# Narrow norm sums spread by DMA, no loop, and the key-value products on DVE, in a one-core RWKV-7 layer with experts

## Chip, cores and metric

One core of one Trainium2 chip runs the whole kernel. The metric is the time of one execution on the device, in microseconds (us). Its engines are TensorE (PE, matrix products; PEld is its weight load), VectorE (DVE), ScalarE (ACT), GpSimd (POOL) and SyncE (SP), which only issues DMA transfers. Each engine runs its own instructions in program order, and they wait for one another by semaphores.

## The reference

The input x has 16 sequences of 512 tokens with 128 channels, that is 16 heads of 8 channels. One layer of RWKV-7 comes first, then a top-1 mixture of 4 experts.

```python
x = _ln(x, ...); xn = _ln(x, ...)              # two layer norms over 128 channels
xr, xw, xk, xv, xa, xg = xn + (_shift(xn) - xn) * x_r, ...
r = xr @ W_r; k = xk @ W_k; v = xv @ W_v
w_log = -softplus(-(w0 + tanh(xw @ w1) @ w2)) - 0.5
a = sigmoid(a0 + xa @ a1 @ a2); g = sigmoid(xg @ g1) @ g2
kk = (k * k_k) / norm(k * k_k over each head); k = k * (1 + (a - 1) * k_a)
def step(state, inp):                          # 512 steps, state is 8x8 for each sequence and head
    sa = einsum('bhij,bhj->bhi', state, a_t)
    state = state * d_t + sa * b_t + v_t * k_t
    return state, einsum('bhij,bhj->bhi', state, r_t)
o = _gn_heads(o) + (r * k * r_k).sum(-1) * v   # norm over each head's 8 channels
x = x + (o * g) @ W_o
x = x + square(relu(kf @ W_ffn1)) @ W_ffn2     # kf: layer norm and shift of x
# then: layer norm, router, top-1 expert of 4 (128 to 512, gelu, 512 to 128), add, layer norm
```

## The kernel before

Channels lie on the 128 partitions. A tile of 512 columns holds one chunk: 32 tokens (steps) of 16 sequences. There are 16 chunks and so 512 steps, each of which needs the state of the one before.

**One step** of the scan is four operations in a ring, on tiles of 128 columns. DVE forms `s_a` = state x a_t (L769). PE sums it over each head into `sa_ps` (L338). DVE forms `upd` = sa_ps x b_t (L775) and the next `state` = upd + plus_kv (L779). Beside it POOL forms `plus_kv` = state + kv (L965) for the same step. The product of values and keys, `kv`, is made ahead of time for a quarter of a chunk (8 steps) by `spread_kv` (L930), in four parts of 256 columns on POOL, at every odd step of the quarter before. Its values come from `val_rep`: SP copies `val_c` over the partitions with 8 DMAs for each quarter (`replicate`, L253). POOL also forms `s_r` = state x r_t at every even step (L957), which PE gathers into `o_ps` (L331), 8 products of 128 columns at steps 3, 11, 19 and 27.

**Everything else** (norms, projections, feed-forward, experts) is done for whole chunks, in slices between the steps: the front of the next chunk and the back of the two before. The table `AT` gives each item a step relative to its chunk's first; item `at` of chunk c stands in every engine's program at step `at` mod 32, between `s_a` and `upd` on DVE, behind the step's `sa_ps` product on PE, behind `plus_kv` on POOL (`pipeline`, L221). ACT and SP have no scan work, so for them `AT` sets only the order. A late input of such an item holds up the scan behind it.

**Norms.** Six times in a chunk (the layer norms `rs0`, `rs1`, `frs`, `ers`, `lrs`, and `rk`, the norm of kk) ACT squares 512 columns, PE sums them over the channels with a full 128x128 weight (`j0`, `j1`, `fj`, `ej`, `lj`, `kks`), which repeats the sum on all partitions, and ACT takes Ln and Exp of all 512 columns (`rsqrt`, L514) into `rs_p`, `rs_m` or `rs_f`. A seventh norm, `grs`, is over heads.

**The loop.** Chunks -1 to 3 and 14 to 17 are written out, chunks 4 to 13 run in a hardware loop of 5 passes over two chunks (L237); -1, 16 and 17 are the fill and drain of the pipeline. Before the first item PE, ACT and POOL wait for all 37 constants (L302, L512, L927), among them the weights that PE transposes and centres (L303 to L319).

Of the kernel before, what the change touches and what calls it, by code (L numbers as in the profile page):

```python
# [25 lines left out]
LOOP_START = 4  # L26

AT = {
    "c0": -32, "x_in": -29, "sq0": -28, "j0": -23, "rs0": -22, "x1": -21, "xh0": -20, "c1": -20, "sq1": -20,
    "j1": -19, "rs1": -17, "xh1": -17, "xn": -15, "dx": -15, "wa": -14, "mix_r": -14, "mix_k": -13, "k": -13,  # L30
    "th_w": -12, "mix_v": -12, "key": -12, "w2": -12, "th_d": -12, "val_c": -11, "mix_g": -11, "rk": -11,
    "v": -10, "kks": -10, "k2": -10, "val_sb": -10, "p": -10, "val": -9, "cum": -9, "rep": (-9, 11, 12, 15),
    "r": -8, "rec": -8, "g1": -8, "kk": -8, "rkb": -7, "k_t": -7, "kki": -7, "a_t": -7, "rkb_ps": -5,
    "th_g": -4, "r_t": -4, "bonus": -4, "g2": -1, "b_t": 0, "bonus_b": 0, "gate": 1, "gsq": 29, "grs": 33,
# [11 lines left out]
CONSTS = 37  # L46
# [60 lines left out]
def build(nc, xT, mats, vecs, consts, b1_in, out):  # L107
    with ExitStack() as ctx:
# [36 lines left out]
        def v(name):  # L145
# [14 lines left out]
        sq_p, lv_p, rs_p, xh_p = (sb(n, COLS) for n in ("sq_p", "lv_p", "rs_p", "xh_p"))  # L160
# [60 lines left out]
        def pipeline(eng, work, scan_step=None):  # L221
# [23 lines left out]
        def _(sp):  # L245
# [4 lines left out]
            for n in range(3):  # L250
                sp.dma_start(b1_rows[32 * n:32 * n + E, :], b1_in).then_inc(s["w_in"], 16)
# [812 lines left out]
```

## Time and profile before

| | |
|---|---|
| median of 3 runs | 1262.86 us (1260.15 to 1266.98) |
| the profiled execution | 1263.76 us, its span 1261.6 us |
| busy share of the span | PE 85%, DVE 70%, POOL 67%, ACT 53% |
| first step of the scan begins | 63.4 us |
| scan ends | 1184.8 us |
| mean granted clock of TensorE | 0.912 of full speed |

The span counts from the first instruction of the program to the last. An engine's share is an average over a start, 16 chunks and a tail. Since the scan is a ring of four dependent operations, the view that tells most is the timeline between one `s_a` and the next: it shows which engine the ring waited for in that step.

### The profile page before, as it was taken

The numbers are of one execution on the slowest core, as the hardware profiler recorded it, in microseconds if no ns is written. First come the engines' busy times: TensorE is split into PE (matmuls) and PEld (weight loads), VectorE is DVE, ScalarE is ACT, GpSimd is POOL, SyncE is SP. The second block draws the span as 40 slices with busy tenths as digits, with TensorE's granted clock in tenths as the row PEclk, the third lists the DMA queues.
The fourth block names the chain that finished last, engine by engine and source line by source line (L and its number), as shares of the span: only waits on it lengthen the run. The fifth ranks groups of instructions, "written<-read, shape, count | busy, mean of one in ns | idle before, by whom it ended". The sixth has DMA issues, their size and how long they took to land.

```text
span 1261.6 us, 17218 instructions
## 1 busy us (share of the span) xinstructions
PE 1069.5 (85%) x4211; PEld 528.6 (42%) x4211; DVE 878.1 (70%) x2155; ACT 665.9 (53%) x967; POOL 845.0 (67%) x1141
## 2 busy tenths in 40 slices
PE   2556688989898998989799998989899998988877
PEld 1133334444444444444444444444444444444433
DVE  3256686877878686877778786787778687876421
ACT  1524173746566383746557383647557383744352
POOL 0167676868777776878677776878677677877210
PEclk9967598989899898989899897989899898989898
DMA  2222212131312212031311212131311213131000
GB/s 103 39 37 51 34 36 35 17 73 17 69 25 53 40 17 63 15 74 17 72 21 45 47 17 59 17 75 17 64 28 44 48 17 64 17 63 17 17 9 8
DMA packets 81165, 49.87 MB, mean 40 GB/s; under 512 B 9148, under 2 KB 74684, under 8 KB 80968
## 3 DMA queue, kind: packets, MB, share of 16 engines
q1 hardware_dynamic: 81096, 49.17, 19.7%
q14 instruction: 52, 0.43, 0.1%
q8 instruction: 17, 0.28, 0.1%
HBM read 11.38 MB, written 4.19 MB: 12 GB/s over the span
## 4 chain that ended last, share of the span: by engine, by line
PE 66%; DVE 22%; issue 6%; ACT 4%; DMA 1%; SPq 0%; POOL 0%; DVEq 0%; ACTq 0%; POOLq 0%
PE sa_ps L338 12%; PE pre_a L298 9%; PE fin_a L479 8%; PE fin_b L479 8%; PE pre_b L298 6%; DVE state L779 6%; DVE s_a L769 5%; DVE upd L775 4%; PE mid_ps L298 4%; PE fin_b L488 3%; PE mid_ps L433 3%; PE fin_a L298 2%; PE o_ps L331 2%; PE fin_b L457 1%; PE fin_b L298 1%
## 5 line engine op out<-in xcount | busy, mean ns | idle before, releaser
L965 POOL TENSOR_TENSOR plus_kv<-state,kv 128x128 f32<-128x128 f32 x512 | 282.0, 551 | 258.2 <-DVE state L779 233.2
L338 PEld LDWEIGHTS sa_ps<-s_a,con 128*128 128x128 f32 x1024 | 191.1, 208 | 352.0 <-DVE s_a L769 267.6
L338 PE MATMUL sa_ps<-s_a,con 128*128 128x128 f32 x1024 | 242.8, 322 | 82.1 <-DVE s_a L769 79.6
L775 DVE TENSOR_TENSOR upd<-sa_ps,b_t 128x128 f32<-128x128 f32 x512 | 147.9, 289 | 198.5 <-PE sa_ps L338 190.0
L942 POOL TENSOR_TENSOR kv<-val_rep,k_t 128x256 f32<-128x256 f32 x256 | 232.4, 908 | 33.3 <-DMA val_rep<-val_c 33.3
L957 POOL TENSOR_TENSOR s_r<-state,r_t 128x256 f32<-128x256 f32 x256 | 225.3, 880 | 1.3 <-DVE state L779 1.3
L779 DVE TENSOR_TENSOR state<-upd,plus_kv 128x128 f32<-128x128 f32 x512 | 190.1, 371 | 19.4 <-POOL plus_kv L965 2.0
L769 DVE TENSOR_TENSOR s_a<-state,a_t 128x128 f32<-128x128 f32 x512 | 177.0, 346 | 19.1 <-DVE state L779 1.7
L479 PE MATMUL fin_b<-h_e,mat 128*128 128x512 f32 x256 | 133.3, 630 | 2.0 <-ACT pick L678 2.0
L508 ACT ACT_TABLE_LOAD x103 | 132.1, 1283 | 1.8
L479 PE MATMUL fin_a<-h_e,mat 128*128 128x512 f32 x256 | 126.5, 599 | 0.0
L678 ACT ACTIVATE pick<-fin_b 68x512 bf16<-68x512 bf16 x16 | 9.5, 592 | 145.9 <-PE fin_b L465 145.9
L633 ACT ACTIVATE sq_m<-o_ps 128x512 f32<-128x512 f32 x16 | 9.6, 597 | 132.2 <-PE o_ps L331 132.2
L488 PE MATMUL fin_b<-act,mat 128*128 128x512 f32 x128 | 66.4, 604 | 0.0
L479 PEld LDWEIGHTS fin_b<-h_e,mat 128*128 128x128 f32 x256 | 48.1, 207 | 42.2 <-issue 39.4
L433 PE MATMUL mid_ps<-hid,mat 128*128 128x512 f32 x128 | 65.5, 594 | 0.3 <-ACT hid L663 0.3
L685 ACT ACTIVATE act<-fin_b 128x512 f32<-128x512 f32 x32 | 19.0, 595 | 79.6 <-PE fin_b L482 79.6
L479 PEld LDWEIGHTS fin_a<-h_e,mat 128*128 128x128 f32 x256 | 44.1, 190 | 36.2 <-issue 33.0
L298 PE MATMUL pre_b<-sq_p,con 128*128 128x512 f32 x96 | 53.5, 641 | 3.0 <-ACT sq_p L526 2.1
L298 PE MATMUL mid_ps<-z_m,mat 128*128 128x512 f32 x96 | 51.0, 614 | 1.3 <-DVE z_m L862 1.3
L983 POOL TENSOR_TENSOR k<-key,k 128x512 f32<-128x512 f32 x16 | 23.0, 1441 | 35.4 <-ACT k L592 35.4
L331 PE MATMUL o_ps<-s_r,con 128*32 128x128 f32 x1024 | 43.0, 288 | 0.0
(189 smaller groups left out, 1791.9 us busy)
## 6 DMA issues: line engine op xcount, KB each, us to landing
val_rep<-val_c SPq DMA_DIRECT2D x512, 64.0 KB, 2.4
x_in<-xT SPq DMA_DIRECT2D x16, 256.0 KB, 2.8
x_res<-xT SPq DMA_DIRECT2D x16, 256.0 KB, 2.9
outT<-res SPq DMA_DIRECT2D x16, 256.0 KB, 2.0
mat<-mats SPq DMA_DIRECT2D x1, 2306.0 KB
con<-consts SPq DMA_DIRECT2D x1, 584.0 KB, 3.6
hid<-b SPq DMA_DIRECT2D x3, 8.0 KB
vec<-vecs SPq DMA_DIRECT2D x1, 11.5 KB, 3.6
```

What stands on the lines that cost most here:

```text
L298: return mm(bank_, lhsT, rhs, start=True, stop=True).then_inc(s[name], 1)
L338: mm(sa_ps[:, 0:STATE], k("sum8"), s_a[:], start=True, stop=True).then_inc(s["sa"], 1)
L433: last = mm(mid_ps[:], w("ffn2", j), hid[j][:], start=(j == 0), stop=(j == J - 1))
L479: mm((fin_b, fin_a)[j % 2][:], mat[:, M["W1"] + e * I + j * C:M["W1"] + e * I + (j + 1) * C], h_e[e][:], start=(e == 0), stop=False)
L488: last = mm(fin_b[:], w("Wo", j), act_j[j][:], start=(j == 0), stop=(j == J - 1))
L508: nc.scalar.preload_act_table_set(name)
L769: tt(ib(s_a[:]), ib(st(t)), over_i(a_t[c.slot][:, t * B:(t + 1) * B]), ALU.mult).then_inc(s["s_a"], 1)
L775: tt(ib(upd[:]), ib(sa_ps[:, 0:STATE]), over_i(b_t[c.slot][:, t * B:(t + 1) * B]), ALU.mult).then_inc(s["upd"], 1)
L779: tt(st(t + 1), upd[:], plus_kv[:, (t % 2) * STATE:(t % 2 + 1) * STATE], ALU.add).then_inc(s["state"], 1)
L942: tt(to, values, keys.unsqueeze(1).broadcast_to([128, 2, QUARTER, B]), ALU.mult).then_inc(s["kv"], 1)
L957: tt(part, states, r.unsqueeze(2).broadcast_to([128, 2, N, B]), ALU.mult).then_inc(s["s_r"], 1)
L965: tt(plus_kv[:, (t % 2) * STATE:(t % 2 + 1) * STATE], st(t), kv[:, at:at + STATE], ALU.add).then_inc(s["plus_kv"], 1)
```

## The change

Five things are changed.

1. **Narrow sums.** The six norms' sums are taken with weights of 32 columns (`mean32`, `sum8k`), four products of 128 columns side by side on the four column groups of PE (`sums`). The result for 512 columns lies on 128 partitions x 128 columns. ACT takes Ln and Exp of 128 columns (`rsqrt_row`) into a small tile, and SP spreads it over the channels with four DMAs (`over_channels`). DVE then waits for these.
2. **No loop.** All iterations are written out.
3. **kv on DVE.** `spread_kv` moves from POOL to DVE, in two halves of 512 columns, at steps 2 and 5 of each quarter.
4. **Start.** `x` is loaded first, the small tiles are filled before the constants arrive, and the weights are turned and centred (`turn_weights`, `center_weights`, `weights`) behind the first items of chunk 0, no longer ahead of them.
5. **A new table** `AT`. `grs` also moves to the bank `mid_ps`.

```diff
+    "c0": -32, "j0": -31, "x_in": -31, "sq0": -30, "rs0": -29, "d_rs0": -24, "xh0": -24, "x1": -24, "c1": -22,
...
+    "gg": 39, "wo": 40, "x2": 41, "fc": 41, "fsq": 41, "fj": 42, "frs": 43, "xf": 45, "d_frs": 45, "x2x": 47,
...
-            with eng.Fori(LOOP_START, LOOP_START + RING * (loops - 1) + 1, RING) as first:
...
+            for c in range(FIRST, LAST + 1):
                 iteration(Chunk(0, c))
...
+            def over_channels(c, name, to, free=(), heads=None):
...
+                sp.wait_ge(s["row_" + name], now)
+                for g in range(4):
...
+                        rows = row[name][32 * g:32 * g + 32, :].unsqueeze(1).broadcast_to([32, 4, QCOLS])
+                        sp.dma_start(to[:, g * QCOLS:(g + 1) * QCOLS], rows).then_inc(s[name], 16)
...
+            def sums(bank_, first, which, of, name):
+                for g in range(4):
+                    last = mm(bank_[32 * g:32 * g + 32, first:first + QCOLS], k(which, 0, 32),
+                              of[:, g * QCOLS:(g + 1) * QCOLS], start=True, stop=True, skip_group_check=True)
...
-                    one(pre_b[:], k("mean"), sq_p[:], "j0")
+                    sums(pre_b, 0, "mean32", sq_p, "j0")
+                    if not c.has(1):
+                        turn_weights()
...
+            def rsqrt_row(c, var, eps, n_in, n_ln, name, scale=1.0):
...
+                f(row[name][:], var, ACT.Ln, bias=eps, scale=scale).then_inc(s[n_ln], 1)
+                act.wait_ge(s[n_ln], c.count())
+                f(row[name][:], row[name][:], ACT.Exp, scale=-0.5).then_inc(s["row_" + name], 1)
...
+            def spread_kv(c, q, half):
...
+                tt(part, values.rearrange("p (i t b) -> p i t b", i=N // 2, t=QUARTER),
+                   keys.unsqueeze(1).broadcast_to([128, N // 2, QUARTER, B]), ALU.mult).then_inc(s["kv"], 1)
...
+                if part in (2, 5) and nxt[0].has():
+                    spread_kv(*nxt, part // 3)
```

**POOL, six steps inside a chunk, before.** `kv` is the key-value product, `s_r` the read-out; `plus_kv` is the scan's own.

```order
L957 TENSOR_TENSOR s_r<-state,r_t1 128x256 [waits s_o,s_r_t]
L965 TENSOR_TENSOR plus_kv<-state,kv 128x128 [waits s_state]
L942 TENSOR_TENSOR kv<-val_rep1,k_t1 128x2x8x16
L965 TENSOR_TENSOR plus_kv<-state,kv 128x128 [waits s_state]
L957 TENSOR_TENSOR s_r<-state,r_t1 128x256
L965 TENSOR_TENSOR plus_kv<-state,kv 128x128 [waits s_state]
L942 TENSOR_TENSOR kv<-val_rep1,k_t1 128x2x8x16 [waits s_val_rep1]
```

And now, at the same kind of place:

```order
L1003 TENSOR_TENSOR s_r<-state,r_t0 128x256
L1011 TENSOR_TENSOR plus_kv<-state,kv 128x128 [waits s_state] x2
L1003 TENSOR_TENSOR s_r<-state,r_t0 128x256 [waits s_o]
L1011 TENSOR_TENSOR plus_kv<-state,kv 128x128 [waits s_state] x2
L1003 TENSOR_TENSOR s_r<-state,r_t0 128x256
L1011 TENSOR_TENSOR plus_kv<-state,kv 128x128 [waits s_state]
```

The product is gone from between two `plus_kv`; only `s_r` is left, at every other one.

**DVE, a chunk's step 25, before.** Between `s_a` and `upd` stand the front of the next chunk (`k_t`, `mix_g`, `a_t`) and `y1` of the back.

```order
L769 TENSOR_TENSOR s_a<-state,a_t1 128x128 [waits s_state]
L820 TENSOR_TENSOR k_t0<-k2,dec_bt 128x512 [waits s_inv_p,s_k2]
L825 SCALAR_TENSOR_TENSOR mix_g<-mix_v,half_kk,dec_bt 128x512 [waits s_g1,s_inv_p,s_kk]
L829 SCALAR_TENSOR_TENSOR a_t0<-mix_v,neg_kk,p_all0 128x512 [waits s_p,s_kk]
L870 TENSOR_TENSOR y1<-mid_ps,x2x 128x512 [waits s_ec,s_y1b,s_x2x,s_f2]
L775 TENSOR_TENSOR upd<-sa_ps,b_t1 128x128 [waits s_sa]
L779 TENSOR_TENSOR state<-upd,plus_kv 128x128 [waits s_plus_kv,s_upd]
```

And now at steps 29 and 30, where the crowded step of the new order is:

```order
L824 TENSOR_TENSOR s_a<-state,a_t0 128x128 [waits s_state]
L811 TENSOR_TENSOR kv<-val_rep0,k_t1 128x4x8x16
L886 SCALAR_TENSOR_TENSOR mix_g<-mix_v,half_kk,dec_bt 128x512 [waits s_g1,s_inv_p,s_kk]
L979 SCALAR_TENSOR_TENSOR res<-y2,vec,y1b 128x512 [waits s_stored,s_y1b,s_lxh]
L834 TENSOR_TENSOR upd<-sa_ps,b_t0 128x128 [waits s_sa]
L838 TENSOR_TENSOR state<-upd,plus_kv 128x128 [waits s_plus_kv,s_upd]
L824 TENSOR_TENSOR s_a<-state,a_t0 128x128 [waits s_state]
L894 SCALAR_TENSOR_TENSOR b_t1<-dx,mix_g 128x512 [waits s_th_a,s_kki]
L834 TENSOR_TENSOR upd<-sa_ps,b_t0 128x128 [waits s_sa]
```

Where step 25 held four operations there is now one (`k_t`), and step 29 holds three, the first of them the second half of a `kv`.

**PE, steps 19 and 20, before**: the shifted projection of the next chunk (`xn` with `mat` and `wa_past`).

```order
L338 MATMUL sa_ps<-s_a,con 128x128 [waits s_s_a]
L298 MATMUL fin_a<-z_m,mat 128x512 [waits s_act,s_kf]
L298 MATMUL mid_ps<-z_m,mat 128x512 [waits s_relu,s_kf]
L338 MATMUL sa_ps<-s_a,con 128x128 [waits s_s_a]
L366 MATMUL pre_a<-xn,mat 128x512 [waits s_xh1,s_xn]
L367 MATMUL pre_a<-xn,wa_past 128x512
L338 MATMUL sa_ps<-s_a,con 128x128 [waits s_s_a]
```

And now at step 16:

```order
L363 MATMUL sa_ps<-s_a,con 128x128 [waits s_s_a]
L397 MATMUL pre_a<-xn,mat 128x512 [waits s_xh1,s_xn]
L398 MATMUL pre_a<-xn,wa_past 128x512
L511 MATMUL fin_a<-h_e1,mat 128x512
L511 MATMUL fin_a<-h_e2,mat 128x512
L363 MATMUL sa_ps<-s_a,con 128x128 [waits s_s_a]
```

The projection has moved in front of two products of the experts, and one step now holds four products of 512 columns behind the scan's own.

## Rows read from the trace of the kernel before

**Rows 1.** Four stretches: length, busy us of PE, PEld, DVE, ACT, POOL, granted clock, DMA.

```profile
203.00:273.60 70.60, 64.26 (x263) 32.19 (x262) 54.74 (x132) 40.95 (x60) 53.02 (x71) 0.94 0.22 42
...
414.20:486.90 72.70, 65.32 (x267) 32.26 (x265) 54.24 (x132) 41.42 (x61) 53.33 (x71) 0.92 0.23 44
...
1054.60:1124.10 69.50, 63.68 (x263) 31.90 (x262) 54.46 (x133) 40.94 (x60) 53.19 (x71) 0.94 0.21 39
...
1184.80:1261.60 76.80, 61.23 (x164) 26.35 (x164) 14.01 (x26) 32.09 (x44) 4.62 (x5) 0.88 0.02 7
```

**Rows 2.** Timeline of two steps at full clock: start us, us, engine, line, operation.

```profile
995.33 0.29 DVE L769 TENSOR_TENSOR s_a<-state,a_t 128x128 f32<-128x128 f32 x1
...
995.68 0.49 PE L338 MATMUL sa_ps<-s_a,con 128*128 128x128 f32 x2 [0.17 <-DVE s_a L769]
...
996.00 1.88 PE L479 MATMUL fin_a<-h_e,mat 128*128 128x512 f32 x4
...
996.86 0.29 DVE L769 TENSOR_TENSOR s_a<-state,a_t 128x128 f32<-128x128 f32 x1
...
997.72 0.39 PE L338 MATMUL sa_ps<-s_a,con 128*128 128x128 f32 x2
...
998.79 0.29 DVE L769 TENSOR_TENSOR s_a<-state,a_t 128x128 f32<-128x128 f32 x1
```

**Rows 3.** Timeline, a step with a two-input operation of 512 columns on DVE.

```profile
612.58 0.29 DVE L769 TENSOR_TENSOR s_a<-state,a_t 128x128 f32<-128x128 f32 x1
...
612.79 0.94 DVE L912 TENSOR_TENSOR y<-y,rs_f 128x512 f32<-128x512 f32 x1
...
613.15 1.17 POOL L957 TENSOR_TENSOR s_r<-state,r_t 128x256 f32<-128x256 f32 x1
...
614.50 0.29 DVE L769 TENSOR_TENSOR s_a<-state,a_t 128x128 f32<-128x128 f32 x1
```

**Rows 4.** Timeline, a product of 512 columns on POOL beside DVE.

```profile
1003.54 1.33 POOL L1001 TENSOR_TENSOR z_m<-z_m,gate 128x512 f32<-128x512 f32 x1
1003.78 1.24 DVE L769 TENSOR_TENSOR s_a<-state,a_t 128x128 f32<-128x128 f32 x1
```

**Rows 5.** DVE and POOL by line and shape, chunks 13 and 14 (984.4 to 1124.1).

```profile
L779 DVE TENSOR_TENSOR state<-upd,plus_kv 128x128 f32<-128x128 f32 x64 | 23.6, 368 | 2.2
L769 DVE TENSOR_TENSOR s_a<-state,a_t 128x128 f32<-128x128 f32 x65 | 22.8, 350 | 2.4
...
L942 POOL TENSOR_TENSOR kv<-val_rep,k_t 128x256 f32<-128x256 f32 x32 | 29.8, 932 | 3.4 <-DMA val_rep<-val_c 3.4
```

**Rows 6.** Timeline, sixteen passes of the read-out's gather on PE.

```profile
1007.43 0.65 PE L331 MATMUL o_ps<-s_r,con 128*32 128x128 f32 x16
```

**Rows 7.** Edge of the loop: timeline, and the list of waits for the whole span.

```profile
486.62 0.29 DVE L765 TENSOR_TENSOR state<-state,p_all 128x128 f32<-128x128 f32 x1 [2.72 <-issue]
...
DVE state L765 <- issue: 11.0, 4, 3.0
```

**Rows 8.** SP's transfers in the timeline, and the list of DMA issues.

```profile
603.41 5.04 SPq L265 DMA_DIRECT2D val_rep<-val_c  x8
...
val_rep<-val_c SPq DMA_DIRECT2D x512, 64.0 KB, 2.4
```

**Rows 9.** Start: timeline, and the first step in the view of tile s_a.

```profile
23.39 2.08 PE L298 MATMUL pre_a<-x_in,con 128*128 128x512 f32 x2 [0.38 <-DVE val_scan L753]
...
53.30 0.63 ACT L519 ACTIVATE rs_p<-lv_p 128x512 f32<-128x512 f32 x1
...
L769 DVE TENSOR_TENSOR s_a<-state,a_t x512: 291/292/1249, 63.4 to 1183.0; 128x128 f32<-128x128 f32 x171
```

**Rows 10.** Tail: pieces of the chain that ended last, in order of time.

```profile
1185.36 5.96 PE fin_b L479 x8
...
1256.96 0.64 ACT rs_f L519
```

**Rows 11.** Granted clock in a stretch of 2.1 us at a chunk's end.

```profile
1052.50:1054.60 2.10, 1.88 (x4) 1.11 (x5) 1.65 (x6) 0.00 (x0) 1.16 (x2) 0.50 0.00 0
```

More of the change, by code:

```diff
@@ new lines @@
+    "gate": 0, "bonus": 0, "bonus_b": 13, "x_res": 33, "gsq": 36, "gj": 36, "grs": 36, "gxh": 38, "gaff": 39,
+    "gg": 39, "wo": 40, "x2": 41, "fc": 41, "fsq": 41, "fj": 42, "frs": 43, "xf": 45, "d_frs": 45, "x2x": 47,
+    "fxh": 48, "hid": (51, 51, 55, 61), "kf": 52, "f1": (52, 53, 54, 55), "f2": (56, 57, 57, 58), "d_ers": 58,
+    "y1": 59, "ec": 59, "ej": 59, "esq": 61, "ers": 62, "h": 63, "router": 63, "best": 64, "onehot": 64,
+    "masks": 64, "h_e": (65, 65, 67, 68), "pick": 65, "y1b": 65,
@@ L157, in build @@
         xf_now, xf_past, x2x = sb("xf_now", COLS), sb("xf_past", B + COLS), single("x2x", COLS)
-        sq_p, lv_p, rs_p, xh_p = (sb(n, COLS) for n in ("sq_p", "lv_p", "rs_p", "xh_p"))
+        sq_p, rs_p, xh_p = (sb(n, COLS) for n in ("sq_p", "rs_p", "xh_p"))
+        row = {n: sb(f"row_{n}", QCOLS) for n in ("rs0", "rs1", "rk", "frs", "ers", "lrs")}
         dx = sb("dx", COLS)
@@ L358, in work @@
                     one(pre_a[:], k("center"), x1[c.slot][:], "c1")
+                    if not c.has(1):
+                        center_weights()
                 if at == AT["j1"]:
@@ L361, in work @@
                     pe.wait_ge(s["ln0"], c.count())
-                    one(pre_b[:], k("mean"), sq_p[:], "j1")
+                    sums(pre_b, 0, "mean32", sq_p, "j1")
                 if at == AT["wa"]:
+                    if not c.has(1):
+                        pe.wait_ge(s["made"], MADE)
                     pe.wait_ge(s["xn"], c.count())
@@ L418, in work @@
                 if at == AT["fj"]:
+                    if c.has(1):
+                        pe.wait_ge(s["fln"], (c + -1).count())
                     pe.wait_ge(s["fsq"], c.count())
                     pe.wait_ge(s["gln"], c.count())
-                    one(var_ps[:], k("mean"), sq_m[:], "fj")
+                    sums(var_ps, 0, "mean32", sq_m, "fj")
                 for j in range(J):
@@ L443, in work @@
                         pe.wait_ge(s["lln"], (c + -1).count())
-                    one(fin_b[:], k("mean"), sq_f[:], "ej")
+                    sums(fin_b, 0, "mean32", sq_f, "ej")
                 if at == AT["router"]:
@@ L493, in work @@
                     pe.wait_ge(s["y2"], c.count())
-                    one(fin_b[:], k("mean"), sq_f[:], "lj")
+                    sums(fin_b, 0, "mean32", sq_f, "lj")
             pipeline(nc.tensor, work, scan_step)
@@ L670, in work @@
                     tables(EXP)
[L671 to L673 removed]
+                    rsqrt_row(c, fin_b[:, 0:QCOLS], eps_ln, "ej", "eln", "ers")
                 if at == AT["pick_sb"]:
@@ L787, in work @@
                     tt(xh_p[:], pre_a[:], rs_p[:], ALU.mult).then_inc(s["xh0"], 1)
+                    if not c.has(1):
+                        weights()
                 if at == AT["xh1"]:
-                    dve.wait_ge(s["rs1"], c.count())
+                    dve.wait_ge(s["rs1"], c.count(64, 64))
                     dve.wait_ge(s["x1"], c.count())
```

291 lines of the change are left out of this document (142 added, 149 removed), and 3 rows, old and new, of the table AT.

## The prediction

> **What bounds the kernel now.** I read three views, in this order. The stretches by chunk come first [rows 1]: a chunk that is written out takes 69.5 to 70.6 us, one in the loop up to 72.7, and in both PE is busy for some 64 of them, DVE for 54, POOL for 53. No engine is full, so the ring of the scan has to be looked at step by step. The timeline of two steps is the second view [rows 2]. The first takes 996.86 - 995.33 = 1.53 us with nothing else on DVE: that is the bare ring, 32 x 1.53 = 49 us a chunk. The second has two products of 512 columns (four passes, 996.00 to 997.72, so 0.86 each) queued on PE behind the first step's `sa_ps`; the next `sa_ps` can start only at 997.72, 0.86 after its `s_a`, where it took 0.35 before, and the step takes 1.93. The other 21 us of a chunk are steps of this kind, and steps where DVE has more than fits. The third view is the timeline of such a step [rows 3]: one operation of 512 columns with two inputs in SBUF, 0.94 long beside POOL's `s_r`, makes it 1.92. POOL also stops DVE outright: beside its product of 512 columns an `s_a` takes 1.24 in place of 0.29 [rows 4]. So three engines take turns at bounding a step, and an item costs only what it adds to the longest side of its own step.
>
> **Prices from these rows.** Per step, beside the 1.53: up to 1.3 us of products on PE are free (1.53 less the 0.22 that `sa_ps` occupies), so one is free, two cost 0.4, three 1.3, four 2.1. On DVE one operation of 0.69 fits, since it lies between `s_a` and `upd`; a second costs 0.7; one of 0.94 beside `s_r` costs 0.4. A product of 512 columns on POOL costs up to 0.9.
>
> **The loop.** At an edge DVE waits 2.72 us before the carried state, and such waits sum to 11.0 us over four edges [rows 7]. Chunks 4 to 13 run from 343.3 to 1054.6, 71.1 us each; the three written-out chunks, 2, 3 and 14, take 69.9 on average. Without the loop: 10 x 1.2 = **-12 us**.
>
> **Start.** The first step begins at 63.4 us, 40 us after the first product at 23.39 [rows 9]. That product no longer waits for the weights. It needs `x` and the constants, which I put at 5.5, so 18 us go. Three norms (`rs0`, `rs1`, `rk`) now have a hop by DMA in the chain. One hop is four issues on SP of 5.04/8 = 0.63 each and 2.4 to land the last [rows 8], 3 x 0.63 + 2.4 = 4.3. Three are 13. Back come some 0.7 on ACT and 0.5 to 1.1 on PE for each, together 4 to 5. The turning of the weights on PE stands before the second sum (+2), the first quarter's `val_rep` now queues on SP behind the third hop, and `kv` and `b_t` come ahead of the first step (+2 to +4). The chain from 53.30, where `rk`'s Exp starts, shows how short the rest is. Sum: -18 + 13 - 4.5 + 2 - 1 = **-8.5 us**, first step at 55.
>
> **A chunk.** Six full sums go, 6 x 0.86 = 5.2 us of PE. Six narrow ones come. The nearest row is the read-out's gather, sixteen passes of 128 columns with 32-column weights in 0.65 at its longest and 0.58 to the next start [rows 6], so eight passes are 0.29, 1.7 us in all. PE loses 3.4 of 64 us. ACT loses 6 x 0.7 = 4, which hides. POOL loses the `kv` products, 29.8/2 = 14.9 us of 53 [rows 5]. DVE gets 8 operations of 0.69 to 0.94, 5.5 to 7.5 us. In return its `state` and `s_a`, which take 0.368 and 0.350 on average but 0.292 undisturbed [rows 5, 9], can shrink: 32 x (0.076 + 0.058) = 4.3 us at most, and only where POOL's `kv` was what disturbed them.
>
> I summed the 32 steps of both orders with the prices above, each step as the longer of its DVE and its PE side, with what PE has left over carried on. Before, this gives 68.1 us against the 69.9 measured. After, it gives 68.3. The crowded steps only move: step 25 with four operations on DVE (4.7) is gone, but step 0 holds `bonus` and the router's comparisons (3.2), 17 three mixes (3.3), 22 the scan of decays and `y2` (3.1), 29 the half `kv` and two more (3.5). On PE step 16 has four products and 7 and 21 three, where before 19, 24, 25 and 26 had three. Of the eight half `kv`, those at steps 13, 18, 21 and 29 lie beside PE work that is as long; those at 2, 10 and 26 meet `s_r` and cost 0.4 each, the one at 5 some 0.2. If none of the eight had cover they would cost 8 x 0.4 = 3.2.
>
> Waits are not in that sum. So I followed one chunk through ACT and SP too, and three inputs come late for the engine that needs them: PE at step 24 waits for the third `hid` (+0.8), PE at step 27 for the square behind `ec`, with the next `sa_ps` queued behind it (+1.2), and DVE at step 16 for `frs` (+0.9). That walk gives 68.7. The sum with its shortfall of 1.8 gives 70.1. I take the middle, 69.4, so -0.5 a chunk and, for the 14 chunks with front and back work, **-6 us**.
>
> SP issues 56 DMAs of 64 KB in a chunk, no longer 32: 56 x 0.63 = 35 of 69 us. They fit, but each hop stands in line. In the walk the margin is about 1 us for `lrs` at step 28 and `rk` at 23, 2 for `ers` at 31, over 3 for `rs0`; `rs1` at 15 comes late by 0.5 under the cover of PE.
>
> A rule of the Trainium skill bears on the POOL side. GPSIMD Engine Reference, Key points, says that GpSimd shares its SBUF interfaces with VectorE and contends with DVE instructions that have two SBUF inputs; the 1.24 of `s_a` [rows 4] agrees. It gives no price, and the same rule speaks against the change, since each `kv` on DVE is now such an instruction itself and meets `plus_kv` and `s_r`. By the rule alone the sum could fall anywhere between the 3.2 us lost and the 4.3 us gained for each chunk.
>
> **Tail.** The scan ends at 1184.8, 76.8 us before the end [rows 1]. Before, the experts of chunk 14 start 0.6 us after that [rows 10]. Now their router runs at step 31, so comparisons, masks and `pick` lie behind the scan's end: they start some 4.4 later. `frs` is covered by the experts' products, `ers` and `lrs` of chunk 15 are not: 2 x (4.3 - 0.9) = 6.8 (the last Exp at 1256.96 had only 4.6 us behind it, a hop more now). PE's narrow sums and a shorter wait for the feed-forward give 2 back. **+9 us**.
>
> **Sum.** Against the profiled execution: 1263.8 - 12 - 8.5 - 6 + 9 = 1246.3, so 1246. The median of three runs, 1262.9, is 0.9 us below that execution, so 1246 is 1.3% below it. About 0.5% is what a measurement of this kernel can tell from no change.
>
> **The rivals.**
>
> *POOL's relief counts in full.* If `state` and `s_a` shrink by half of the 4.3 us on the path, a chunk takes 67.3: 1246 - 14 x 2.1 = 1217. For it: the 512-column stops [rows 4] come where POOL runs behind. Against: most of those operations stay on POOL, and `s_r` too. 15%.
>
> *The `kv` halves have no cover and nothing comes back.* 70.4 us a chunk, +1.0: 1260, no change. For it: DVE is at 54 of 70 us [rows 1] and gets some 6 more. 17%.
>
> *The hops come late* (this one ends slower). If a hop takes 1.3 us longer than 4.3, because SP is held by a `val_rep` of 8 issues (5.04 us) or by a wait in its order, `rs1`, `frs`, `rk` and `lrs` all stop DVE, whose `upd` and so the ring stand behind them: 1.3 + 1.3 + 0.5 + 0.3 = 3.4 a chunk, 1246 + 14 x 3.4 = 1294. It decides from a lateness of about 0.6 us, where the gain is gone. Against it: SP stood idle most of the time. 15%.
>
> *PE's clock falls for longer.* At a chunk's end the granted clock is 0.50, the 1.2 GHz level [rows 11]; before it PE had little to do in steps 28 and 29. Now steps 28 to 30 hold one product each, one of them in 3.5 us, and steps 8 to 12 hold about one each. At half clock `sa_ps` gives its result 0.2 later and one product is 1.7 long, so such a step costs 0.2 to 0.6. Four or five more of them are 2 us a chunk: 1274. TensorE: Matmul & The Clock Gate, Part 1 of the Trainium skill, says that the throttled clock is the default and activity releases it; by that, taking work off PE gives something back. 10%.
>
> *The change doesn't do what it says*, `kv` on DVE standing still for `val_rep` that SP issues late: the same price as late hops, within that 15%.
>
> **Chances.** The forecast (1225 to 1256) 43%, the rivals 15, 17, 15 and 10. Low end: the first rival, 1217. High end: the clock, 1274, and half of the late hops, 1282. Faster by over 0.5% (below 1256.5): 43 + 15 and a little of the third, 60%. Within: 16%. Slower: 24%.
>
> **What would show it.** First `s_a` at 53 to 58 us; written-out chunks of 68 to 71; no DVE wait by "issue" before the carried state; `kv` on DVE at 0.69 to 0.94 mean; `rs_p`, `rs_m`, `rs_f` transfers landing 4.3 us after their first issue, with no DVE wait for them over 1 us but at step 16; a tail of 83 to 89. Chunks above 71.5, or DVE waiting for DMA in every chunk, would make me wrong.

## The result, and the profile after

The changed kernel takes **1223.4 us**, median of 4 runs (1222.3 to 1228.2); the kernel before takes 1264.1 beside it. The ratio is 0.969, with a 95% interval of 0.965 to 0.973: 3.1% faster, where 1.3% was forecast. The time lies inside the range given, but the gain is more than twice the forecast one.

The profiled execution has a span of 1221.7 us, 39.9 less than before. The first `s_a` of chunks 0, 2 and 15 and the end of the scan cut both spans into the same pieces:

| piece | before | after | difference | forecast |
|---|---|---|---|---|
| start, to the first step | 63.4 | 52.7 | -10.7 | -8.5 |
| chunks 0 and 1 | 139.6 | 132.4 | -7.2 | |
| chunks 2 to 14 | 921.1 | 885.2 | -35.9 | -18 for chunks 0 to 14, 12 of it the loop |
| chunk 15 | 60.7 | 60.7 | 0 | |
| tail | 76.8 | 90.7 | +13.9 | +9 |

The stretches of the changed kernel: its length, then the busy us of PE, PEld, DVE, ACT and POOL, the granted clock, and what the DMA did. Chunk 2, chunk 8, chunks 2 to 14 together, and the tail:

```profile
185.10:251.90 66.80, 59.07 (x299) 28.28 (x298) 58.49 (x141) 37.36 (x60) 42.44 (x55) 1.00 0.34 68
592.50:660.90 68.40, 61.57 (x299) 30.39 (x299) 58.49 (x141) 37.10 (x60) 42.45 (x55) 0.95 0.33 66
...
185.10:1070.30 885.20, 793.58 (x3873) 389.10 (x3872) 761.41 (x1820) 482.89 (x780) 551.36 (x715) 0.96 0.33 66
...
1131.00:1221.70 90.70, 64.49 (x214) 29.83 (x213) 16.34 (x36) 27.03 (x42) 4.61 (x5) 0.80 0.07 18
```

Against [rows 1], POOL went from 53 to 42 us a chunk and DVE from 54 to 58. A chunk takes 68.1 on average, where the written-out ones before took 69.5 to 70.6. Chunks 2 and 8 hold the same instructions, but chunk 2 ran wholly at the higher clock (1.00) and took 1.6 us less. The steps that differ are 1 (3.28 against 2.05) and 31 (2.22 against 1.92). What the lower clock costs is what the prediction left out, as the experiments show.

The scan's own operations on DVE and the moved product, in chunks 13 and 14 (busy us, mean ns; idle before):

```profile
L838 DVE TENSOR_TENSOR state<-upd,plus_kv 128x128 f32<-128x128 f32 x64 | 24.6, 384 | 2.2
L824 DVE TENSOR_TENSOR s_a<-state,a_t 128x128 f32<-128x128 f32 x64 | 18.7, 292 | 2.3
L811 DVE TENSOR_TENSOR kv<-val_rep,k_t 128x512 f32<-128x512 f32 x16 | 15.1, 944 | 0.0
```

`s_a` fell from 350 to its floor of 292 [rows 5]. `state` did not follow, it rose from 368 to 384. Each half of `kv` takes 0.94, the upper of the two prices given.

Where chunk 8 loses against chunk 2 is seen in the timeline (start, us, engine, line, operation). Chunk 2, steps 1 and 2, at the higher clock:

```profile
187.13 0.62 PE L489 MATMUL fin_b<-ident_bf,onehot 128*128 128x128 bf16 x8
...
187.59 0.61 PE L489 MATMUL fin_a<-ident_bf,onehot 128*128 128x128 bf16 x8
187.63 0.29 DVE L824 TENSOR_TENSOR s_a<-state,a_t 128x128 f32<-128x128 f32 x1
...
188.03 0.44 PE L363 MATMUL sa_ps<-s_a,con 128*128 128x128 f32 x2
...
189.68 0.29 DVE L824 TENSOR_TENSOR s_a<-state,a_t 128x128 f32<-128x128 f32 x1
```

The same place in chunk 8, at the lower one:

```profile
595.09 0.29 DVE L824 TENSOR_TENSOR s_a<-state,a_t 128x128 f32<-128x128 f32 x1
...
595.43 1.06 PE L489 MATMUL fin_b<-ident_bf,onehot 128*128 128x128 bf16 x8
...
596.28 1.05 PE L489 MATMUL fin_a<-ident_bf,onehot 128*128 128x128 bf16 x8
...
597.13 0.47 PE L363 MATMUL sa_ps<-s_a,con 128*128 128x128 f32 x2
...
598.37 0.29 DVE L824 TENSOR_TENSOR s_a<-state,a_t 128x128 f32<-128x128 f32 x1
```

The one-hot products stand ahead of step 1's `sa_ps`. At the lower clock they take 1.06 in place of 0.62 and begin later (the product of `x_in` ahead of them takes 2.04 in place of 1.10), so `sa_ps` starts 2.04 after its `s_a`, no longer 0.40, and the step takes 3.28 in place of 2.05: 1.2 us lost in one step.

### The profile page after: what moved, and what is told of

It is laid out like the page before. It is cut to its first block, busy times and chain, and to the rows that moved or that the text cites. A ratio compares the mean times of both kernels' runs of the same rounds, so it can differ in the third digit from the quotient of the medians.

```text
span 1221.7 us, 16912 instructions
## 1 busy us (share of the span) xinstructions
PE 1023.8 (84%) x4787; PEld 500.2 (41%) x4787; DVE 947.1 (78%) x2283; ACT 604.0 (49%) x965; POOL 675.1 (55%) x885
## 4 chain that ended last, share of the span: by engine, by line
PE 52%; DVE 27%; ACT 10%; issue 7%; DMA 2%; SPq 2%; DVEq 0%; ACTq 0%
PE sa_ps L363 10%; PE fin_a L511 8%; PE fin_b L511 8%; DVE state L838 7%; DVE upd L834 5%; PE pre_a L314 5%; DVE s_a L824 4%; PE fin_b L520 4%; DVE kv L811 3%; PE mid_ps L314 3%; PE o_ps L356 2%; ACT hid L695 2%; PE fin_a L314 2%; ACT hid L697 1%; PE mid_ps L465 1%
## 5 line engine op out<-in xcount | busy, mean ns | idle before, releaser
L363 PEld LDWEIGHTS sa_ps<-s_a,con 128*128 128x128 f32 x1024 | 179.5, 203 | 385.3 <-DVE s_a L824 331.4
L1003 POOL TENSOR_TENSOR s_r<-state,r_t 128x256 f32<-128x256 f32 x256 | 259.6, 1014 | 1.3 <-DVE state L838 1.3
L838 DVE TENSOR_TENSOR state<-upd,plus_kv 128x128 f32<-128x128 f32 x512 | 197.7, 386 | 17.5
L824 DVE TENSOR_TENSOR s_a<-state,a_t 128x128 f32<-128x128 f32 x512 | 149.4, 292 | 18.5
L811 DVE TENSOR_TENSOR kv<-val_rep,k_t 128x512 f32<-128x512 f32 x128 | 120.2, 940 | 3.0 <-DMA val_rep<-val_c 3.0
L511 PE MATMUL fin_a<-h_e,mat 128*128 128x512 f32 x256 | 122.3, 593 | 0.0
L520 PE MATMUL fin_b<-act,mat 128*128 128x512 f32 x128 | 67.5, 614 | 0.0
L511 PEld LDWEIGHTS fin_b<-h_e,mat 128*128 128x128 f32 x256 | 43.7, 198 | 27.0 <-issue 24.5
L575 ACT ACTIVATE x<-xh_p,vec 128x512 f32<-128x512 f32 x16 | 13.0, 814 | 79.2 <-DVE x L913 63.8
L702 ACT ACTIVATE sq_f<-fin_a 128x512 f32<-128x512 f32 x16 | 9.6, 597 | 75.1 <-PE fin_a L314 75.1
L567 ACT ACTIVATE sq_p<-pre_a 128x512 f32<-128x512 f32 x16 | 9.6, 597 | 67.2 <-PE pre_a L314 67.2
```

What stands on the lines that cost most here:

```text
L363: mm(sa_ps[:, 0:STATE], k("sum8"), s_a[:], start=True, stop=True).then_inc(s["sa"], 1)
L511: mm((fin_b, fin_a)[j % 2][:], mat[:, M["W1"] + e * I + j * C:M["W1"] + e * I + (j + 1) * C], h_e[e][:], start=(e == 0), stop=False)
L520: last = mm(fin_b[:], w("Wo", j), act_j[j][:], start=(j == 0), stop=(j == J - 1))
L811: tt(part, values.rearrange("p (i t b) -> p i t b", i=N // 2, t=QUARTER), keys.unsqueeze(1).broadcast_to([128, N // 2, QUARTER, B]), ALU.m ...
L824: tt(ib(s_a[:]), ib(st(t)), over_i(a_t[c.slot][:, t * B:(t + 1) * B]), ALU.mult).then_inc(s["s_a"], 1)
L838: tt(st(t + 1), upd[:], plus_kv[:, (t % 2) * STATE:(t % 2 + 1) * STATE], ALU.add).then_inc(s["state"], 1)
```

## The experiments

Each kernel was timed beside the kernel before on the same chip. "A chunk" below is the length from the first `s_a` of chunk 2 to that of chunk 15, divided by 13.

### Without the loop

```diff
-            with eng.Fori(LOOP_START, LOOP_START + RING * (loops - 1) + 1, RING) as first:
-                for n in range(RING):
-                    iteration(Chunk(first, n))
+            for c in range(FIRST, LAST + 1):
+                iteration(Chunk(0, c))
```

> The kernel before with chunks 4 to 13 written out, nothing else changed. The changed kernel took 43 us less over chunks 0 to 14; the question is how much of that is the loop. If the loop costs what the prediction said (11.0 us of waits at its edges and a little inside), this runs at 1250 to 1253 us, chunks 4 to 13 take 69.9 each and chunks 0 to 3 and 14 don't change. If the loop also slows the ten chunks inside it, it is 1243 or less. If the waits at the edge only hide others, 1260.

Measured: 1249.0, ratio 0.989 (0.986 to 0.993). Chunks 2 to 14 of the kernel before, and of this one:

```profile
203.00:1124.10 921.10, 832.52 (x3407) 415.34 (x3406) 709.37 (x1717) 531.13 (x780) 691.67 (x923) 0.94 0.21 41
```

```profile
202.40:1109.50 907.10, 831.20 (x3407) 415.95 (x3406) 707.72 (x1717) 532.39 (x780) 691.26 (x923) 0.94 0.22 42
```

They differ by 14.0 us, forecast were 12. The loop term held. What is left for the other parts is 907.1 - 885.2 = 21.9 us, 1.7 a chunk.

### The products of keys and values, in either order

In the order of before (no loop), moved to DVE; and in the changed kernel, moved back to POOL:

```diff
# noloop_kv, on the kernel before without its loop
+                if part in (2, 5) and nxt[0].has():
+                    spread_kv(*nxt, part // 3)                      # DVE, 512 columns
-                if part % 2 == 1 and nxt[0].has():
-                    spread_kv(*nxt, part // 2)                      # POOL, 256 columns
# after_kvpool, on the changed kernel: the same lines the other way round
```

> The kernel before without the loop, and the key-value products on DVE in halves of 512 columns at steps 2 and 5 of each quarter; table, norms and start are the old ones. Theory (POOL's relief is real and needs nothing else): s_a falls to 0.29 and a chunk by 1 to 2 us, 15 to 30 us under the run without the loop. Rival (the new table is what makes room for these products): they cost 0.2 to 0.4 each on the old crowded steps, a chunk goes up by 1 to 3 us and the run is 15 to 40 us above the one without the loop.

> The changed kernel with the key-value products back on POOL, four parts of 256 columns at the odd steps of a quarter; everything else is as changed. If the move to DVE carries the gain in a chunk, a chunk takes 69.8 or more in place of 68.3 and the run 1245 or more. If the table and the narrow sums carry it, the run stays within 6 us of the changed kernel's 1223. A time below 1220 would mean that the move costs.

Measured: 1273.3 for the first, ratio 1.009 (1.006 to 1.012), that is 24 us **slower** than without the move. 1233.9 for the second, ratio 0.978 (0.974 to 0.982), that is 10 us slower than the changed kernel, so there the move gains. Most of that gain lies ahead of the steady chunks: in the traces the two differ by 8.2 us, and 6.8 of them are there at the first `s_a` of chunk 2 (191.9 against 185.1). A chunk gains 0.3. Step 18 of a chunk shows why the old order has no room (first kernel):

```profile
668.80 0.29 DVE L778 TENSOR_TENSOR s_a<-state,a_t 128x128 f32<-128x128 f32 x1
...
669.01 0.94 DVE L765 TENSOR_TENSOR kv<-val_rep,k_t 128x512 f32<-128x512 f32 x1
669.37 1.17 POOL L956 TENSOR_TENSOR s_r<-state,r_t 128x256 f32<-128x256 f32 x1
...
669.88 1.22 DVE L818 SCALAR_TENSOR_TENSOR mix_r<-dx,vec,xn 128x512 f32<-128x512 f32 x1
...
671.65 0.29 DVE L778 TENSOR_TENSOR s_a<-state,a_t 128x128 f32<-128x128 f32 x1
```

`kv` and a mix meet in one step beside `s_r`, and it takes 2.85. In the new table DVE has `kv` alone at step 18, and the step takes 1.92. The rival "no cover" is right about cover in the old order and wrong about the new one. The case that the whole gain is POOL's relief falls too, since `s_a` fell to 292 in the old order too, and that kernel is slower than the one before.

### Wide sums, and both parts undone

```diff
# after_wide
-                    sums(pre_b, 0, "mean32", sq_p, "j0")
+                    one(pre_b[:], k("mean"), sq_p[:], "j0")
-                    rsqrt_row(c, pre_b[:, 0:QCOLS], eps_sq, "j0", "ln0", "rs0", scale=1.0 + 1e-5)
+                    rsqrt(c, pre_b[:], eps_sq, rs_p[:], rs_p[:], "j0", "ln0", "rs0", scale=1.0 + 1e-5)
-                if at == AT["d_rs0"]:
-                    over_channels(c, "rs0", rs_p, [("kk", -1)])
# the same for rs1, rk, frs, ers, lrs; table_start: this, and kv back on POOL
```

> The changed kernel with the six norms' sums wide again: full 128x128 weights, Ln and Exp of 512 columns, no transfers over the channels. If PE's 3.4 us a chunk were on the path in full, a chunk takes 71.7 and the run 1255 less what the start and the tail give back. By the prices of the prediction: a chunk +1.0 (14 us), the three hops of the start away (first step at 44 to 46, -8), two of the tail away (-7): 1222, no change. If the sums bring nothing in a chunk, 1208.

> The changed kernel with both the norms' sums wide and the key-value products back on POOL: against the run without the loop (1249) only the table and the start are new, against the changed kernel (1223) two parts are undone at once. If the parts add up, it is 1223 - 8 (wide sums) + 10.5 (products on POOL) = 1226, and chunks 2 to 14 take 68.7 to 69.3 where they take 69.8 without the loop. If the table needs the products on DVE, they take 69.8 or more and the run is 1238 or more. If the table alone carries the gain of a chunk, they take 68.1 to 68.4.

Measured: 1215.1 with wide sums, ratio 0.962 (0.959 to 0.966), so the kernel is **faster** without the narrow sums, where no change (1222) was forecast by the prices. 1237.4 with both undone, ratio 0.978 (0.973 to 0.982), its runs wide apart (1228.5 to 1239.2). If the parts added up it would be 1226; the median is 11 us above that and a chunk takes 69.7, next to the 69.8 at which the table needs the products on DVE, while the fastest run comes near the 1226. Undoing the sums takes 6 us off the start (first step at 46.8) and 7 off the tail (83.9), and a chunk goes up by 0.8, to 68.9. (The profiled execution is the slowest of four, 4 us above the median, which is 0.3 a chunk.) The granted clock over chunks 2 to 14 is the surprise, 0.99 against 0.96:

```profile
176.00:1071.50 895.50, 811.59 (x3407) 388.67 (x3406) 760.55 (x1820) 531.95 (x780) 551.83 (x715) 0.99 0.22 42
```

With narrow sums PE has less to do and its clock is lower. Before, the mean was 0.94, that is 2 x 0.06 of the time at the lower level, some 8 us of each chunk; in the changed kernel some 5, here 1 to 2. With both parts undone it is some 3 (mean clock 0.98), so the new table and the start alone leave far less of the lower clock than the old order does. Why a given order holds the clock better is not shown beyond where it falls: in the old order over steps 29 to 31, 0 and 1, in the new one over 0 and 1 and at times 31.

### Products that nobody needs

If the clock matters so much, products into unused columns of a bank, placed where PE stands idle at a chunk's end, should pay. They add work and change no result.

```diff
+                if c.has() and c.has(1):
+                    for _ in range({28: 1, 29: 2}.get(t, 0)):       # after_fill; noloop_fill: {25: 2, 28: 2, 30: 1}
+                        mm(var_ps[:, QCOLS:COLS], k("sum8"), con[:, 0:COLS - QCOLS], start=True, stop=True,
+                           skip_group_check=True)
```

> The kernel before without its loop, with five such products in each chunk (two at step 25, two at 28, one at 30). Before, a chunk's sum by steps fell short of the measured chunk by 1.8 us. If the lower clock at its end makes that difference, a chunk falls from 69.8 to about 68.2 and the run from 1249 to 1225 to 1232. If late inputs or POOL make it, the time stays at 1249 or rises by up to 1 us a chunk.

> The changed kernel with three products on PE added to each chunk (384 columns into unused columns of a bank, one at step 28 and two at step 29, where PE stands idle for 1.6 to 1.9 us), to keep the granted clock up. In the changed kernel the clock is at its lower level around a chunk's end and step 1 takes 3.2 to 3.3 us there; with wide sums it mostly stayed up and step 1 took 2.0. If the clock is the cause, step 1 takes 2.0 to 2.2 in nearly all chunks and the run is 10 to 16 us shorter, 1207 to 1213. If it is not, the three products cost 0 to 1 us a chunk: 1223 to 1236.

Measured in the old order: **1229.9**, ratio 0.974 (0.972 to 0.976), 19 us less than without them; a chunk took 68.2. Its chunks 7 and 8:

```profile
546.60:614.60 68.00, 63.69 (x273) 31.52 (x272) 54.48 (x132) 40.95 (x60) 53.16 (x71) 1.00 0.22 43
614.60:684.30 69.70, 65.34 (x273) 32.46 (x272) 54.36 (x132) 40.95 (x60) 53.15 (x71) 0.98 0.22 42
```

Eleven of thirteen look like the first, at clock 1.00 and 68.0 us (one more took 68.1). The one with a fall in it took 69.7.

The 68.0 hold a cost of the added products themselves. Step 26 has the higher clock in both kernels. Without them (chunk 6 of the kernel without the loop):

```profile
536.34 0.29 DVE L763 TENSOR_TENSOR s_a<-state,a_t 128x128 f32<-128x128 f32 x1
...
536.68 0.49 PE L332 MATMUL sa_ps<-s_a,con 128*128 128x128 f32 x2
...
538.26 0.29 DVE L763 TENSOR_TENSOR s_a<-state,a_t 128x128 f32<-128x128 f32 x1
```

With them, two queued at step 25:

```profile
533.45 0.29 DVE L769 TENSOR_TENSOR s_a<-state,a_t 128x128 f32<-128x128 f32 x1
...
533.58 1.45 PE L342 MATMUL var_ps<-con 128*128 128x384 f32 x4
...
534.87 0.38 PE L332 MATMUL sa_ps<-s_a,con 128*128 128x128 f32 x2
...
535.95 0.29 DVE L769 TENSOR_TENSOR s_a<-state,a_t 128x128 f32<-128x128 f32 x1
```

The step takes 2.50 in place of 1.92, and step 29 takes 2.58 in place of 2.46, so the products cost 0.7 of what they bring. Without that cost the old chunk at clock 1.00 is put at 67.3, an estimate from these steps.

In the new order three products were not enough: 1219.4, ratio 0.965 (0.962 to 0.967). That is 4 us less than the changed kernel; the intervals overlap, though each of the four runs is below each of the changed kernel's. The clock rose to 0.98, but was still low over steps 0 and 1 in most chunks, and step 1 kept its 3.2 us. My forecast of 1207 to 1213 was wrong: products at steps 28 and 29 alone don't keep the clock up over steps 0 and 1. The same question was put to the moved `kv` in the old order, with four such products (one at 25, two at 28, one at 30):

> The kernel before without its loop, with the key-value products on DVE in halves, and four added products of 384 columns on PE in each chunk (one at step 25, two at 28, one at 30). Without the added products the move made chunks 2 to 14 1.9 us longer (69.8 to 71.7), and the lower clock lasted 10.3 us in place of 8.6. If the clock is why the move lost, it gains here against the same kernel with the products on POOL (68.2): 68.0 or less, 1228 or less. If the old table has no cover for the products, the difference stays: 69.8 to 70.3 a chunk, 1250 to 1256.

Measured: 1247.1, ratio 0.987 (0.985 to 0.990); a chunk takes 69.6, and 69.2 where the clock stays up. Here the added products cost nothing: at step 26 the kernel with the move takes 2.85 with them and without, since DVE has the longer side there. So at equal clock the old order loses 1.9 us by the move (67.3 to 69.2), the same as at its own clock (69.8 to 71.7). The order is the cause of the loss, and the clock has no part in it that shows.

### The same chunk at the same clock

From these runs every combination has chunks that ran wholly at clock 1.00, in the old order only with added products. One row each for: the moved `kv` in the old order; the table with both parts undone; `kv` on POOL; wide sums.

```profile
338.50:407.60 69.10, 63.07 (x270) 31.26 (x270) 58.99 (x140) 40.88 (x60) 41.53 (x55) 1.00 0.21 42
```

```profile
673.80:742.90 69.10, 61.70 (x263) 29.11 (x263) 55.38 (x133) 40.93 (x60) 52.56 (x71) 1.00 0.22 43
```

```profile
260.00:328.10 68.10, 58.91 (x299) 27.98 (x298) 55.15 (x132) 37.13 (x60) 52.45 (x71) 1.00 0.33 66
```

```profile
313.80:382.20 68.40, 61.74 (x264) 29.32 (x263) 58.50 (x141) 40.95 (x60) 42.50 (x55) 1.00 0.22 43
```

| order | kv on | sums | a chunk at clock 1.00 | mean of chunks 2 to 14 |
|---|---|---|---|---|
| old | POOL | wide | 68.0 with added products, 67.3 less their 0.7 | 69.8 (without) |
| old | DVE | wide | 69.2 (with added products) | 71.7 (without) |
| new | POOL | wide | 69.0 to 69.1 | 69.7 |
| new | DVE | wide | 68.3 | 68.9 |
| new | POOL | narrow | 67.6 to 68.2 | 68.4 |
| new | DVE | narrow | 66.8 | 68.1 |

At equal clock the new table alone costs 1.7 us a chunk (67.3 to 69.0). It pays because `kv` on DVE, which costs 1.9 in the old order, gains 0.8 to 1.4 in it, and the narrow sums gain 0.9 to 1.6. Together 67.3 becomes 66.8. The lower clock then adds 2.5 to the old chunk and 1.3 to the new: 69.8 and 68.1. So of the 1.7 us that a chunk gained beside the loop, 0.5 is work and order, and 1.2 is less of the lower clock.

Some cells are weak. In the old order no chunk ran at clock 1.00 without added products, so 67.3 rests on the 0.7 read from the steps. The 66.8 is one chunk of the changed kernel; a chunk of `after_fill` (66.8) and one of `mixed` (66.7) agree. The means are of one execution each, and the 69.7 is of a slow one among runs that lie 0.8 a chunk apart. Narrow sums were not tried in the old order, and the table and the start were not undone one without the other.

### Later hops

```diff
# after_late: six DMAs for each hop, not four
                 for g in range(4):
+                    for lo, hi in ([(0, 64), (64, QCOLS)] if g < 2 else [(0, QCOLS)]):
```

> The changed kernel with six DMAs instead of four for each norm's hop (two of the four pieces split in two), so that each hop lands 2 x 0.60 = 1.2 us later and SP has 7 us more to issue in a chunk. The prediction's third rival priced such a lateness at 3.4 us a chunk, 48 us in all. In the changed kernel DVE waits 0.5 to 0.6 us for two of the six hops of a chunk, and the others land up to 1.5 us ahead. By the rival 1271; by these waits and margins at most 2 x 1.2 a chunk, and with PE's cover half of that, 1240 to 1250 with the start's 3.6 and the tail's 2.4 in it; if the hops are covered but for start and tail, 1229.

Measured: 1278.9, ratio 1.013 (1.010 to 1.015), a chunk at 71.4, +3.3 against the 3.4 that the third rival was priced at. It comes where the rival put it: step 15 (`rs1`) takes 1.1 more, step 16 (`frs`) 1.4, step 23 (`rk`) 0.7, where the rival had 1.3, 1.3, 0.5 and another 0.3 for `lrs`. My 1240 to 1250 was far off. The waits of DVE in this kernel (us in total, times, longest):

```profile
DVE xh_p L852 <- DMA rs_p<-row_rs: 30.5, 16, 4.3
DVE y_m L917 <- DMA rs_m<-row_frs: 30.0, 15, 9.3
DVE mix_v L877 <- DMA rs_p<-row_rk: 29.7, 16, 7.2
```

and in the changed kernel:

```profile
DVE mix_v L877 <- DMA rs_p<-row_rk: 9.6, 4, 6.1
DVE y_m L917 <- DMA rs_m<-row_frs: 8.9, 4, 8.0
DVE xh_p L852 <- DMA rs_p<-row_rs: 8.7, 15, 2.2
```

Three of the six hops turn into waits of nearly 2 us in every chunk. For `frs` a late hop also puts off the next one on SP: `rs1` and `frs` are issued back to back, as the timeline of the changed kernel shows:

```profile
617.88 2.50 SPq L262 DMA_DIRECT2D rs_p<-row_rs  x4
620.49 2.48 SPq L262 DMA_DIRECT2D rs_m<-row_frs  x4
624.50 0.69 DVE L917 TENSOR_TENSOR y_m<-mid_ps,rs_m 128x512 f32<-128x512 f32 x1
```

For these three the new table has its readers where the hops land, with next to nothing to spare.

### Wide where nothing covers the hop, and a kept clock

`mixed` is the changed kernel with wide sums for the three norms of chunk 0's front and the three of chunk 15's back.

```diff
+        def is_wide(c, name):
+            return c.off == 0 if name in FRONT else c.off == CHUNKS - 1
```

> The changed kernel with wide sums only where no steps cover the transfers: the three norms ahead of the first step (chunk 0) and the three at the end (chunk 15); all others narrow as changed. With all six wide the first step came 6 us sooner and the tail was 7 us shorter, while chunks 2 to 14 took 0.8 more each. If these are separate prices, this runs at 1223 - 6 - 7 = 1210, chunks 2 to 14 at 68.1. If the start and the tail gain less because PE's clock falls there, 1215 to 1218.

Measured: **1209.6**, ratio 0.958 (0.955 to 0.960), the 1210 that was worked out: first step at 46.2, tail 82.5, a chunk 68.1. With six products added in each chunk:

```diff
+                    for _ in range({28: 1, 29: 2, 30: 1, 31: 1}.get(t, 0)):     # and one in step 0, behind c0
```

> The changed kernel with the first and last norms wide (as in the run with both, 1209.6) and six added products of 384 columns on PE in each chunk: one at step 28, two at 29, one each at 30, at 31 and in step 0 behind the centring of x. Three of them, at 28 and 29 alone, shortened the lower clock from 5.2 to 2.9 us a chunk but left it over steps 0 and 1, where step 1 takes 3.2 in place of 2.0. If work on PE right up to there keeps the clock, step 1 takes 2.0 to 2.2 in nearly all chunks, chunks 2 to 14 take 66.8 to 67.2 and the run is 1193 to 1198. If the added products then stand in the way of the next step's sa_ps, 67.5 to 68.5 and 1203 to 1215.

Measured: **1194.7**, ratio 0.946 (0.944 to 0.948), 29 us less than the changed kernel and 5.4% less than before. Chunk 8:

```profile
579.80:647.20 67.40, 62.20 (x311) 30.55 (x310) 58.50 (x140) 37.11 (x60) 42.41 (x55) 1.00 0.34 67
```

All thirteen chunks are like it, 67.3 to 67.5 at clock 1.00. Step 1 takes 2.6, not 2.0, so the added products cost 0.6 of what they bring.

> The run before it (1194.7) without the added product at step 31; five are left, at 28, 29, 29, 30 and in step 0. There the lower clock was gone from chunks 2 to 14, and step 1 took 2.6, not the 2.0 of chunks at the higher clock, since the added products stand in PE's order ahead of the one-hot products of step 0. If the one at step 31 makes this 0.6, step 1 takes 2.0 to 2.2, chunks 2 to 14 take 66.7 to 66.9 and the run is 1187 to 1190. If the one in step 0 makes it, nothing changes (1193 to 1197). If the clock needs the one at step 31, the lower level comes back and step 1 takes 3.2: 1200 or more.

Measured: 1209.6, ratio 0.957 (0.954 to 0.960), as without any. Its chunks 3 and 7:

```profile
247.10:314.40 67.30, 61.85 (x309) 30.33 (x308) 58.56 (x140) 37.10 (x60) 42.52 (x55) 1.00 0.34 67
519.00:588.00 69.00, 63.56 (x309) 31.06 (x309) 58.54 (x141) 37.09 (x60) 42.52 (x55) 0.98 0.33 65
```

The product at step 31 held the clock: without it the clock falls over steps 0 and 1 in six of the thirteen chunks. The one in step 0 makes the 0.6: step 1 takes 2.6 in chunk 3, and 4.3 in chunk 7 where the clock fell with the extra product queued ahead of it.

## Why the prediction was wrong

**What bounds the kernel** was read rightly as a ring that waits in turn for PE, DVE and POOL, and the prices from the rows held: 0.94 for `kv` on DVE, 4.1 for a hop where 4.3 was forecast (from the first issue at 1176.82 to its reader at 1180.88, in the rows on the tail below).

**The loop**, -12: right, 14.0 in the trace and 13.1 by the medians.

**A chunk**, -0.5: this is the step that failed, -1.7 measured. The term that was missing is the lower clock, 2.5 us of the old chunk and 1.3 of the new. Two numbers were wrong with it.

First, "the sum with its shortfall of 1.8 gives 70.1. I take the middle". The sum gave 68.1 for the old chunk, 1.8 under the measured one, and I carried half of that over to the new chunk as an unknown. At clock 1.00 the old chunk takes 67.3, so the shortfall was two errors: the clock's 2.5 left out, less 0.8 by which the steps were priced too high. [rows 11] showed the clock. I had priced it in a rival, as something that might get worse, and left what was already there out of the sum.

Second, the sum for the new order, 68.3, was 1.5 too high against the 66.8 at equal clock. Step 0 was put at 3.2 and takes 2.5 (in chunk 2 from 185.1 to 187.6), 29 at 3.5 and takes 3.0, 17 at 3.3 and takes 3.0. The late inputs at steps 24 (+0.8) and 27 (+1.2), which belong to the walk that gave 68.7, did not come at that size: these steps take 1.9 and 2.0. That 68.3 equals the step times of most chunks is chance, since it leaves out the clock's 1.3. Chance too is that -0.5 is what a chunk gains at equal clock: the sums themselves had +0.2. With the measured figures in their place a chunk is 66.8 + 1.3 = 68.1, 13 x 1.3 = 17 us less than the 69.4 of the forecast, and the whole 1229.

**Chunks 0 and 1** were not costed at all, and gave 7.2 us. By the first `s_a` of chunk 2 the kernel without the loop stands at 202.4, the table and start alone at 184.8, with `kv` moved to DVE as well at 176.0, and with narrow sums too at 185.1. So up to there the start and the table bring 17.6, `kv` on DVE 8.8, and the narrow sums cost 9.1. The 8.8 of `kv` are 12.3 less in chunks 0 and 1 (141.5 to 129.1) against 3.5 more ahead of the first step (43.3 to 46.8). With `kv` on POOL and narrow sums the very first step takes 9.9 us, for the products then stand behind the first `s_a` and no longer ahead of it.

**Start**, -8.5, measured -10.7: near it, but in part by luck. The narrow sums cost 5.9 (first step at 46.8 with wide ones), where 13 - 4.5 = 8.5 was put down for them. The +2 to +4 for `kv` and `b_t` is named and not in the sum, which has a -1 that no row gives; `kv` on DVE costs 3.5. The rest brought 20.1 (63.4 to 43.3, with both parts undone), where -18 + 2 - 1 = -17 stood. The first step of the changed kernel, in the view of tile `s_a` (min/median/max ns, first and last start):

```profile
L824 DVE TENSOR_TENSOR s_a<-state,a_t x512: 277/292/295, 52.7 to 1129.2; 128x128 f32<-128x128 f32 x171
```

**Tail**, +9, measured +13.9. The narrow sums account for 6.8 of it (the tail with wide ones is 83.9), where the terms +6.8 and -2 gave 4.8; the rest, 7.1, was put at 4.4. In the chain that ended last:

```profile
1132.15 0.19 DVE best L942
...
1137.21 2.05 PE fin_b L511 x2
...
1176.82 0.54 SPq L262
...
1178.70 2.16 DMA rs_f<-row_ers
...
1180.88 0.70 DVE h L936
```

The experts' products begin 6.2 us after the scan's end at 1131.0, where it was 0.6 [rows 10]: 5.6 later, not 4.4. The first of them takes 2.05 at the lower clock, where 0.86 is its time at the higher [rows 2]; the tail's mean clock is 0.80, where it was 0.88 [rows 1]. How much of the tail the lower clock makes was not tried.

**The rivals.** "POOL's relief counts in full" named a time, 1217, that came close, but its mechanism is only a part: `s_a` shrank as it says, `state` did not, and the same relief came with a loss of 24 us in the old order. "No cover" is refuted for the new order. "The hops come late" did not happen, and its price for a chunk held when it was made to happen (3.3 against 3.4). "PE's clock falls for longer" had the right mechanism with the wrong sign: it falls for less long, some 5 us a chunk in place of 8 to 9. That is 1.2 of the 1.7 us that a chunk gained beside the loop.

**Smaller slips in the sums.** 14 x 0.5 is 7, not the 6 of "A chunk". At the range's high end half of the late hops gives 1246 + 24 = 1270, not 1282.

The rule of the Trainium skill that I weighed (GPSIMD Engine Reference, Key points, on the SBUF interfaces shared with VectorE) agrees with the 1.22 of `mix_r` beside POOL's `s_r`, where `mix_k` of the same form takes 0.94 a step later (at 671.86). How much of the 24 us lost in the old order is such contention and how much is DVE's own added work was not taken apart, and the rule does not tell which order wins. TensorE: Matmul & The Clock Gate, Part 1, says that the throttled clock is the default and activity releases it; the runs with added products agree, 19 us and 15 us less for nothing but added products. I had cited it for a chance of 10% and should have put it into the sum.

## What to carry over

Price a chunk at one clock, and add the lower clock as a term of its own, with the step that it hits; a sum that falls short of the measured stretch by a constant is a hint at such a term, and should be traced before it is carried over. Products that hold the clock up have a price too, and a chunk measured with them has to be freed of it before it is compared. A move of work between engines has no price of its own: the same `kv` on DVE cost 1.9 us a chunk in one order and gained 0.3 to 0.8 in another, so it is judged with the order that makes room for it. Where a latency has no work beside it, as in a start or a tail, the older and more expensive form can stay there alone.

## What was not expected of the hardware

Products that nobody reads made the kernel faster: five a chunk took the old order from 1249.0 to 1229.9, six took the last kernel from 1209.6 to 1194.7. One product at step 31 decides whether the clock stays up over steps 0 and 1: with it in all thirteen chunks, without it in seven. A single fall at steps 0 and 1 costs 1.2 to 1.7 us, since PE's product of `x_in` and its short one-hot products stand ahead of `sa_ps` there. And POOL's products of 512 columns still stop DVE: in the changed kernel `s_a` never takes over 0.295 us, but `state` rose to 0.384 on average (chunks 13 and 14). The stops that are left have moved to another operation of the ring, as step 7 of the last kernel but one shows (`mixed_fill`, timeline):

```profile
594.65 1.26 POOL L1069 TENSOR_TENSOR z_m<-z_m,gate 128x512 f32<-128x512 f32 x1 [0.63 <-DVE z_m L936]
594.80 1.25 DVE L866 TENSOR_TENSOR state<-upd,plus_kv 128x128 f32<-128x128 f32 x1
```
